# Rows of the hashed experts by quarters: one DMA per half, row 4t+s in block s, and a turn that writes with a stride of four

## The reference, cut to what matters

```
e_idx = token_ids.reshape(N) * HASH_PRIME % E            # E = 16
slot = where(pos < C, e_idx * C + pos, E * C)            # C = N // E = 256
buf = zeros((E * C + 1, D)).at[slot].set(xk_flat)
expert_in = buf[:E * C].reshape(E, C, D)
h = square(relu(einsum('ecd,edf->ecf', expert_in, w_key)))
expert_out = einsum('ecf,efd->ecd', h, w_value)
```

## Time and profile before

| | us |
|---|---|
| median of three runs | 2497.04 |
| profiled execution, its own time | 2495.91 |
| span of its trace | 2494.3 |
| TensorE busy | 2440.2 |
| VectorE busy | 1165.9 |
| TensorE's wait at the entry of the hashed stage | 4.6 |

### The profile page before, as it was taken

The page is one execution under the profiler, slowest core; times in us unless marked ns, Lnnn a source line. Parts: engine busy times, 40 slices in busy tenths (PEclk is TensorE's granted clock), DMA queues, the critical chain, the costliest instruction groups (busy, mean ns, idle before and its releaser), DMA issues. The chain is left out here.

```text
span 2494.3 us, 40938 instructions
## 1 busy us (share of the span) xinstructions
PE 2440.2 (98%) x12427; PEld 2033.9 (82%) x12429; DVE 1165.9 (47%) x1803; ACT 900.0 (36%) x1459; POOL 552.1 (22%) x498
## 2 busy tenths in 40 slices
PE   8999999999999899999999989999999999999999
PEld 4778888888899688888888879988978888888877
DVE  5555455325343343443444357777743233332356
ACT  3233333216555322222222246666642222222234
POOL 1100000002222276657666510000011111111100
PEclk9999999999999999999999999999999999999999
DMA  8698898407566543373345257666741011010035
GB/s 290 201 331 306 302 322 312 161 20 274 163 217 245 177 118 114 110 254 115 110 139 168 89 202 254 229 245 228 257 137 41 25 34 32 27 34 25 25 102 185
DMA packets 149813, 412.82 MB, mean 166 GB/s; under 512 B 31379, under 2 KB 52339, under 8 KB 133218
## 3 DMA queue, kind: packets, MB, share of 16 engines
q1 hardware_dynamic: 122450, 314.21, 36.5%
q0 software_dynamic: 19072, 61.66, 8.1%
q10 hardware_dynamic: 8208, 35.88, 3.7%
HBM read 558.71 MB, written 144.80 MB: 282 GB/s over the span
## 5 line engine op out<-in xcount | busy, mean ns | idle before, releaser
L99 PE MATMUL s_g<-wx_hi,s_x_hi 128*128 128x512 f32 x512 | 203.4, 397 | 2.3 <-DVE s_x_lo L2325 1.6
L101 PE MATMUL s_g<-wx_hi,s_x_lo 128*128 128x512 f32 x512 | 200.2, 391 | 0.0
L100 PE MATMUL s_g<-wx_lo,s_x_hi 128*128 128x512 f32 x512 | 199.5, 390 | 0.0
L2041 DVE TENSOR_TENSOR s_w_lo<-s_w_raw,s_w_hi 128x1024 fp32r<-128x1024 f32 x124 | 146.3, 1220 | 49.7 <-ACT s_w_hi L1970 48.5
L99 PE MATMUL s_g<-s_u,s_c_hi 128*128 128x512 f32 x384 | 152.8, 398 | 1.6 <-PEq L1854 1.6
L99 PE MATMUL s_h_ps<-s_x_hi,s_w_hi 128*128 128x256 f32 x512 | 146.0, 285 | 4.6 <-DVE s_x_lo L2073 4.6
L101 PE MATMUL s_g<-s_u,s_c_lo 128*128 128x512 f32 x384 | 149.9, 390 | 0.0
L100 PE MATMUL s_g<-s_u,s_c_hi 128*128 128x512 f32 x384 | 149.5, 389 | 0.0
L101 PE MATMUL s_h_ps<-s_x_hi,s_w_lo 128*128 128x256 f32 x512 | 145.8, 285 | 0.0
L100 PE MATMUL s_h_ps<-s_x_lo,s_w_hi 128*128 128x256 f32 x512 | 145.8, 285 | 0.0
L2224 POOL DMA_INDIRECT s_y<-mid_hash_out,first_rec x32 | 31.8, 994 | 465.5 <-DMA mid_hash_out<-s_o 381.8
(11 more groups left out here) (409 smaller groups left out, 6808.4 us busy)
## 6 DMA issues: line engine op xcount, KB each, us to landing
s_half<-mid_w ACTq DMA_DIRECT2D x124, 2048.0 KB
s_w_raw<-in_w SPq DMA_DIRECT2D x64, 512.0 KB, 6.2
mid_w<-s_x_grp SPq DMA_DIRECT2D x32, 1024.0 KB, 5.6
mid_w<-s_pool_b SPq DMA_DIRECT2D x32, 1024.0 KB, 4.9
s_half<-mid_w SPq DMA_DIRECT2D x32, 1024.0 KB
s_w_raw<-in_w2h SPq DMA_DIRECT2D x16, 2048.0 KB, 7.4
s_w_raw<-in_w1h SPq DMA_DIRECT2D x15, 2048.0 KB, 7.6
mid_routed<-s_o_sb SPq DMA_DIRECT2D x72, 256.0 KB
```

Source lines behind the costliest of these rows:

```text
L99: pe.matmul(out, a_hi, w_hi, start=first, stop=False, skip_group_check=True)
L100: pe.matmul(out, a_hi, w_lo, start=False, stop=False, skip_group_check=True)
L101: return pe.matmul(out, a_lo, w_hi, start=False, stop=last, skip_group_check=True)
L2041: dve.tensor_tensor(lo[:, c], raw[:, c], hi[:, c], ALU.subtract).then_inc(S[name + "_lo"], 1)
```

## The change

`load_by_quarters` issues one DMA in place of four. Its source is taken as (g, r, c): group g, row r, feature c of the group, written straight over the 128 partitions of the tile. So the partition 32g + t now gets rows 4t, 4t+1, 4t+2, 4t+3 in its blocks s = 0 to 3, in place of rows t, 32 + t, 64 + t, 96 + t. The pieces are still 512 bytes. The semaphore rises by 16 per half in place of 64.

`turn_quarters` must bring the rows back into the order of DRAM. Transposed element t of block s belongs to row 4t + s, so the instruction writes consecutive elements four floats (16 bytes) apart, in place of next to each other.

```diff
 def load_by_quarters(eng, dst, rows, sem):
 
-    for g in range(P // 32):
-        eng.dma_start(dst[32 * g:32 * g + 32].rearrange("t (s c) -> t s c", c=P),
-                      rows[:, g * P:(g + 1) * P].rearrange("(s t) c -> t s c", t=32)).then_inc(sem, 16)
+    eng.dma_start(dst, rows.rearrange("r (g c) -> g r c", c=P)).then_inc(sem, 16)
...
 def turn_quarters(dve, dst, src):
 
-    return dve.transpose(dst.rearrange("p k (s t) -> p k s t", t=32), src.rearrange("p (s k a) -> p k s a", s=4, a=32))
+    return dve.transpose(dst.rearrange("p k (t s) -> p k s t", s=4), src.rearrange("p (s k a) -> p k s a", s=4, a=32))
...
             def turn_x(m):
                 def stage(e):
-                    dve.wait_ge(S[f"x_in{m}"], e * 64 + 64)
+                    dve.wait_ge(S[f"x_in{m}"], e * 16 + 16)
                     wait_for(dve, S[f"x_lo{m}"], e)
                     turn_quarters(dve, xt[:, :, rows(m)], x[:, m]).then_inc(S[f"xt{m}"], 1)
```

## The result

| | before | after |
|---|---|---|
| median, us | 2497.04 | 2509.4 (2508.62 to 2511.36) |
| profiled execution, us | 2495.9 | 2508.62 |
| its span, us | 2494.3 | 2507.0 |

The ratio of after to before is 1.0054, 95% interval 1.0043 to 1.0065. The median grew by 12.4 us, the span by 12.7. The forecast was 2509, with 12.6 us of growth: 10.2 in the steady run and 2.4 at the entry. Each of the runs further down is compared with the kernel before as it was timed beside it, 2495.0 to 2495.3 us.

What follows compares the result with a forecast made beforehand. TensorE, busy 98% of the span, was taken to bound the kernel. Steady turns 10.2 us plus entry 2.4 made 12.6 on 2495.9, so 2508.5; the median of runs 1.1 higher gave 2509, range 2497 to 2522.

Steps and rivals of the forecast that it cites:

- What bounds, and h_lo(3) without slack: Hashed stage: TensorE bounds, busy 98%; h_lo(3) stands behind both turns, so TensorE waits for their growth in every expert.
- The turn, d = 0.34: VectorE's turns, fifteen steady pairs: each turn grows by 0.34 us, 10.2 us in all, bounds 0 and 15.9.
- The bound of 0: Low end for one turn's growth on VectorE: 0 if writes 16 bytes apart are still free.
- Four DMA engines: Loads of x: one DMA per half runs on four of 16 engines, 3.6 us per half, both 7.2.
- The entry, 2.4 us: Start of the hashed stage: second half lands 2.1 us late, plus its turn's own growth, 2.4 us together.
- Issue costs nothing: SyncE's queue: 2 DMAs per expert in place of 8, which took 3.92 us; nothing waits for that, cost nothing.
- the cover of 6 us: SyncE's queue, steady run: the load of w2 behind the x loads leaves 6 us later, when w2_lo lets it.
- The cover of 0.4 us ahead of the second turn: Steady run: x lands at worst at 1646.5, the second turn is due at 1646.93, so 0.4 us is left.
- Free stride: Rival, turns: 16 bytes apart is written at dense rate, no steady wait; 2497 to 2499 us, chance 0.26.
- The crowded case: Rival, steady loads: four busy engines run slower, second turn waits, TensorE pays 15 times; 2518 to 2536 us, chance 0.17.
- The same turns, but no narrowing: Rival, whole kernel: turns grow the same but transfers keep their engines; 10.9 us, 2508, part of the forecast's chance.
- A gain: Rival, SyncE: fewer DMAs give its 3 us back to someone; at most 0 here, chance 0.05.

Runs made afterwards that it cites:

- e7: Changed kernel with two DMAs per half in place of one, each with outer sizes of 2 and 64: 2582.4 us, ratio 1.0343.
- e2: Kernel before with one DMA per half but the turn left dense, rows staying in another order within the half: 2498.7 us, ratio 1.0013.
- e8: Changed kernel with h_lo(3) put between the two turns in VectorE's order: 2499.97 us against 2495.25, ratio 1.0018.
- p1: Kernel before with eleven turns and copies of various steps added at VectorE's end: turns at 8 bytes free, at 16 bytes 0.34 to 0.37 us more.
- e1: Kernel before with the turn written at a stride of four, still four DMAs per half in new row order: 2506.55 us against 2495.01, ratio 1.0046.
- e9: Changed kernel with h_lo(3) between the turns and only expert 0's halves loaded by four DMAs each: 2498.96 us, ratio 1.0012.

## Why the prediction was right, step by step

The mechanism is the one forecast: longer turns paid through h_lo(3) in every expert, and a late second half at the entry. That the total came so close, 12.4 for 12.6, is partly luck: the steady term was 1.0 us too high and the entry's 1.0 to 1.3 too low.

**What bounds, and h_lo(3) without slack:** right. The distance from h_lo(3) to the weight load stayed 0.12 us, and the wait came in every expert.

**The turn, d = 0.34:** the term was 10.2 us and measured 9.2 (0.61 per expert). Two errors cancel in part. The row says 0.40 per turn, over my middle; but instructions overlap on VectorE, and h_lo(3) is only 0.33 per turn later. The bound of 0 holds at 8 bytes and not at 16; the upper one, 0.53, was above anything that a step cost. Of the rows at hand the read 128 bytes apart was the nearest, though it seemed the farthest. The cost is flat from 16 bytes on, and the copy's row was of the wrong kind: at 24 bytes a copy of 512 pays 0.18, less than the 0.26 worked out from the short one. The matmul behind h_lo(3) came 0.63 us later per expert, where about 0.7 was forecast.

**Four DMA engines:** borne out twice, by the share (0.25 to 0.29) and by e7. The second half was forecast in 9.0 us behind the start of the loads (1.8 + 7.2). It was in 8.8 behind it here (1464.96 to 1473.72), and 9.5 and 9.9 behind it in e2 and e8. The rate per engine, if four carry it, is 21.8 GB/s alone and not 18.3; but from 1466.4 to 1473.7 both halves averaged 17.9, with a slow start (56 and 68 GB/s) and other traffic from 1470.0 on. So the sum held by two things that it didn't have.

**The entry, 2.4 us:** too low. From the start of the loads it is 11.41 against 9.08, so 2.33, but that match sets an execution at full speed against one at the slow clock. With like clocks it is 3.4 and 3.7, and the wait itself grew by 3.9. That the slow clock of the entry "stays about as long" had no ground, since it comes and goes between executions of the same program.

**Issue costs nothing:** right in its effect, wrong as told. I priced SyncE's two issues as less work than the eight. In the steady run the two take longer than the eight took. SyncE's queue in the same steady expert, beside the earlier trace rows:

```profile
1640.81 6.88 SPq L106 DMA_DIRECT2D s_x<-mid_hash_in  x2
1647.92 2.77 SPq L1928 DMA_DIRECT2D mid_hash_out<-s_o  x1
1650.88 0.34 SPq L1922 DMA_DIRECT2D s_w_raw<-in_w2h  x1
```

6.88 us against 3.92, and the store behind them 2.77 against 0.37. As I read it, SyncE is held while four engines work off what they were given; in e7 four issues took about 12.7. The load of w2 now leaves at once behind the store, so the cover of 6 us that I named is gone. Against the turns it leaves 0.7 us later (19.07 behind them, 18.37 before); it lands in 9.1 us by the page where the earlier trace rows had 7.4, and no wait for it appears. I can't say how near that is.

```profile
s_w_raw<-in_w2h SPq DMA_DIRECT2D x16, 2048.0 KB, 9.1
```

**The cover of 0.4 us ahead of the second turn:** far too small. The DMA view of 1640 to 1656 us (slices of 0.4 us), where x is issued from 1640.81:

```profile
DMA  9209737999989989612222222223999369797797
GB/s 384 82 0 451 164 123 287 410 410 492 410 369 532 410 369 532 287 31 82 87 87 87 87 87 87 85 86 92 358 507 333 128 219 445 246 553 328 328 614 328
```

The rate of x alone ends at about 1651.2, and the second turn is due at about 1656.1 (the pair starts at 1655.14). So, as I read it, x was in some 5 us early; the forecast had put the worst case at each step.

**The rivals.** Free stride is out by p1 and by the turn's rows. The crowded case didn't come: no turn waited for a DMA in the steady run, and it does come in e7, at half the rate; nothing between the two was tried. "The same turns, but no narrowing" gave 2508 in the prediction, and e1 is that kernel: 2506.55 when before read 2495.01, so 11.5 us more, where the prediction had 10.9. A gain was not seen. Among the versions tried none beats the kernel before; the best with the strided turn is e9, 0.12% slower.

## What to carry to other kernels

Price a longer instruction by what stands behind it in its engine's order and by that one's slack, then check what takes over: h_lo(3) between the turns gave back most of the steady cost, h_lo(3) first little more than half (3.9 of the 9.2 us stayed), because ScalarE's work came into the open. Fewer DMAs are not cheaper ones: state a transfer with outer sizes on both sides that share a large factor, or it runs on few engines and holds the issuing queue as well. And measure a wait against a fixed event and not by its length alone, since its beginning can move with the clock; then compare executions that had the same clock there.

## What the runs showed of the hardware

- VectorE, 128x512 in fp32: a turn costs 0.70 us dense and at a step of 8 bytes, 0.81 at 12, 1.04 at 16, 1.02 at 24, 1.07 at 32. Copies: 0.41, 0.41 at 8, 0.49 at 12, 0.59 at 16 and 24.
- Transfers in pieces of 512 bytes ran at 87 GB/s when stated as 4 by 128, at 44 when stated as 2 by 64: 22 GB/s per engine, an estimate that takes four and two engines to carry them.
- An issue can take long: two DMAs stated as 4 by 128 held SyncE for 6.88 us in a steady expert, up to 8.9 for one elsewhere, and a plain store behind them took 2.77 where 0.37 is usual.
- Eight DMAs of 64 KB took 3.69 us to issue with one order of rows on the DRAM side and 5.19 with another. Why was not tried.
- The granted clock over the same 8 us ahead of the hashed stage was 0.79 in some executions and 1.00 in others, with the kernel before too; TensorE's last product there ended 4.47 and 2.91 us behind the start of the loads.
